# Layer 2 attention: six products of bf16 parts in 48 rows, two heads in the two halves of TensorE's rows

## The reference, cut to what matters

```
qkv = x @ w_qkv
q, k, v = split(qkv, 3)                 # each to (B=2, H=16, S=1024, dh=8)
q, k = rope(q), rope(k)
scores = einsum('bhqd,bhkd->bhqk', q, k) * dh ** -0.5
scores = where(tril(ones(S, S)), scores, finfo.min)
out = einsum('bhqk,bhkd->bhqd', softmax(scores), v)
return out @ w_out
```

## Time and profile before

| | |
|---|---|
| Runs | median 1307.3 us of 3 (1306.64 to 1309.63) |
| Profiled execution | 1312.35 us; its span, first to last instruction, 1311.1 us |
| TensorE busy over the span | 957.8 us (73%) |
| VectorE busy over the span | 916.1 us (70%) |
| ScalarE busy over the span | 570.3 us (43%) |
| Mean granted TensorE clock | 0.852 |
| Layer 2 attention, first maxima matmul to last pv | 545.5 to about 846 us |

### The profile page before, as it was taken

How to read it: one execution, slowest core, us unless ns; L and a number is a source line. 1 busy time by engine, 2 the same in 40 slices (tenths; PEclk the granted TensorE clock), 3 DMA queues, 4 the chain that set the end, 5 groups by cost and what they waited for, 6 DMA issues and landing times.

```text
span 1311.1 us, 18576 instructions
## 1 busy us (share of the span) xinstructions
PE 957.8 (73%) x5191; PEld 568.2 (43%) x5191; DVE 916.1 (70%) x1714; ACT 570.3 (43%) x1212; POOL 554.6 (42%) x553
## 2 busy tenths in 40 slices
PE   6957787878665866589999998768897381258782
PEld 3412233333344542233444433248897250247682
DVE  7599999999899557477777774184444579982223
ACT  3264564566032343216666666524343481123222
POOL 2037996899401324211111111125543487225553
PEclk9868998999778887559999999758999595659897
DMA  8000000000000300720221110051111100011113
GB/s 282 0 0 1 0 0 1 1 0 1 1 0 1 129 1 0 160 43 17 41 39 36 28 36 2 0 227 38 38 34 38 51 1 1 0 36 42 39 34 111
DMA packets 28689, 49.45 MB, mean 38 GB/s; under 512 B 7856, under 2 KB 15544, under 8 KB 27568
## 3 DMA queue, kind: packets, MB, share of 16 engines
q1 hardware_dynamic: 23344, 37.81, 10.2%
q0 software_dynamic: 4096, 8.35, 2.0%
q10 hardware_dynamic: 1152, 2.10, 0.4%
HBM read 37.61 MB, written 12.58 MB: 38 GB/s over the span
## 4 chain that ended last, share of the span: by engine, by line
PE 44%; DVE 29%; issue 10%; ACT 6%; POOL 5%; DMA 3%; SPq 1%; another core or an unknown queue 0%; DVEq 0%; ACTq 0%; POOLq 0%
PE ps L2710 9%; PE ps L1734 6%; PE ps L1719 5%; PE ps L2719 5%; PE ps L1671 5%; POOL sb_gs L889 4%; DVE sb_hs L750 3%; DVE sb_l_mxp L1848 2%; DVE sb_xn L168 2%; DVE sb_stats L145 2%; PE ps L588 1%; ACT sb_l_rc L2140 1%; PE ps L1675 1%; PE ps L471 1%; DVE sb_l_pr L2260 1%
## 5 line engine op out<-in xcount | busy, mean ns | idle before, releaser
L1848 DVE TENSOR_REDUCE sb_l_mxp<-ps 128x2 f32<-128x1024 f32 (+3 forms) x152 | 173.8, 1166 | 62.4 <-PE ps L1671 60.3
L889 POOL TENSOR_TENSOR sb_gs<-sb_hs,sb_xp 128x512 f32<-128x512 f32 x128 | 161.4, 1280 | 28.7 <-DVE sb_hs L750 26.4
L1791 ACT ACTIVATE sb_l_pT<-ps 128x512 f32<-128x512 f32 (+3 forms) x256 | 113.2, 506 | 97.5 <-PE ps L1719 94.9
L2710 PE MATMUL ps<-sb_hT,sb_f_shared 128*128 x936 | 127.4, 288 | 13.9 <-ACT sb_f_shared L2727 6.7
L588 PE MATMUL ps<-sb_gs,sb_ident 128*128 128x512 f32 x256 | 133.7, 605 | 1.0 <-POOL sb_gs L889 0.7
L2710 PEld LDWEIGHTS ps<-sb_hT,sb_f_shared 128*128 128x128 f32 x936 | 116.4, 200 | 22.9 <-issue 22.8
L2780 DVE SCALAR_TENSOR_TENSOR sb_f_rows<-ps,sb_f_mask,sb_f_rows 128x128 f32 x78 | 27.3, 351 | 114.5 <-PE ps L2719 50.2
L2808 POOL DMA_INDIRECT moe_y<-sb_f_rows,sb_f_rowi x64 | 64.1, 1002 | 81.8 <-DVE sb_f_rows L2780 71.2
L2719 PE MATMUL ps<-sb_sw_f_out,sb_f_hid 128*128 x624 | 86.6, 283 | 11.4 <-issue 10.1
L849 ACT ACTIVATE sb_xp<-ps 128x512 f32<-128x512 f32 x96 | 57.2, 596 | 85.6 <-POOL sb_gs L889 62.3
L2749 ACT ACTIVATE sb_f_hid<-ps 128x512 f32<-128x512 f32 x78 | 46.5, 596 | 100.8 <-PE ps L2710 80.9
(11 more groups left out here) (400 smaller groups left out, 2116.4 us busy)
## 6 DMA issues: line engine op xcount, KB each, us to landing
sb_sw_f_in<-w_f_in SPq DMA_DIRECT2D x2, 2048.0 KB, 9.8
sb_sw_f_out<-w_f_out SPq DMA_DIRECT2D x2, 2048.0 KB, 12.7
sb_l_qk<-spill SPq DMA_DIRECT2D x18, 192.0 KB
sb_l_qk<-spill SPq DMA_DIRECT2D x54, 64.0 KB
spill<-sb_l_parts SPq DMA_DIRECT2D x12, 256.0 KB, 4.3
moe_y<-c_f_zero SPq DMA_DIRECT2D x1, 2048.0 KB, 9.8
sb_sw_f_up<-w_f_up SPq DMA_DIRECT2D x1, 2048.0 KB, 13.1
moe_h<-sb_f_rows SPq DMA_DIRECT2D x8, 256.0 KB, 4.8
```

The source lines that it names most:

```text
L889: gp.tensor_tensor(gs[:, q % SL, :], hs[:, q % SL, :], cs[:, k % 2, hf * CH:(hf + 1) * CH], ALU.mult).then_inc(times_c, 1)
L1791: ac.activation(pT[e % 3][:, h, 0:width], ps[:, 4 + n_bank % 3, 0:width], ACT.Exp, scale=L2_SCALE).then_inc(exped, 1)
L1848: dv.tensor_reduce(dst, src, AX_X, ALU.max).then_inc(max_out, 1)
L2710: m = pe.matmul(ps[:, 2 * (i % 2) + n, fs], own[:, i % 2, n, fs], xr[:, bass.ds(r, 1), :], start=True, stop=True)
```

## The change

Of the nine products only six are kept: part a of q with part d of k for a + d of at most 2 (`PARTS`). They fill R = 48 rows, 51 with the maxima's rows. Two heads of a set now lie side by side, one from partition 0 and one from partition 64 (HALF), in two slots each, so that a set's matmuls come in pairs: the same slot and tile, rows 0 to 50 for one head and rows 64 to 114 for the other. The results of a pair go to two different PSUM banks. The mask matmuls keep all 128 rows; there are two for each group that needs them. All three buffers now have storage of their own and all their ones are set ahead of the loop, one GpSimd memset over all partitions for each buffer. A stack is 18 DMAs (was 12), a set's rows of maxima 6 DMAs (was 3). The order of the steps, the groups and what VectorE reduces in each are as before.

```diff
-        R = 9 * DH
+        PARTS = [(0, 3), (1, 2), (2, 1)]
+        R = 6 * DH
+        HALF = P // 2
         HG = 4
+        SLOTS = HG // 2
...
-        qk2 = sb("l2_qk", [R + 3, 2, 2, HG, S], BF16, ctx=ctx)
-        third = parts[0:R + 3].rearrange("p j d n -> p (j d n)")[:, 0:2 * HG * S].rearrange("p (j g n) -> p j g n", j=2, g=HG)
-        qs = [qk2[:, 0, 0], qk2[:, 1, 0], third[:, 0]]
-        ks = [qk2[:, 0, 1], qk2[:, 1, 1], third[:, 1]]
+        qk3 = sb("l2_qk", [P, NB3, 2, SLOTS, S], BF16, ctx=ctx)
+        qs = [qk3[:, i, 0] for i in range(NB3)]
+        ks = [qk3[:, i, 1] for i in range(NB3)]
...
-        CONST, STACKED, MAXROW, SPILLED, MX, MP = 5, 12 * 16, 3 * 16, 6 * 16, 1, 6
+        CONST, STACKED, MAXROW, SPILLED, MX, MP = 6, 18 * 16, 6 * 16, 6 * 16, 1, 6
...
-                def score(bank, col, width, h, t, key, start, stop):
-                    return pe.matmul(ps[:, b0 + bank, col:col + width], qs[i][0:R, h, t * P:(t + 1) * P],
-                                     ks[i][0:R, h, key:key + width], start=start, stop=stop)
...
+                def both(col, width, slot, t, key, start, stop):
+                    for half in range(2):
+                        rows = slice(half * HALF, half * HALF + R)
+                        m = pe.matmul(ps[:, b0 + half, col:col + width], qs[i][rows, slot, t * P:(t + 1) * P],
+                                      ks[i][rows, slot, key:key + width], start=start, stop=stop)
                     return m
+                def masks(blocks):
+                    for half in range(2):
+                        out = ps[:, b0 + half, :].rearrange("p (u n) -> p u n", n=P)[:, 0:HG:blocks, :]
+                        pe.matmul(out, idb[:], tri[:].unsqueeze(1).to_broadcast([P, HG // blocks, P]), start=True, stop=False)
...
-                    _, t, _, key, width, pair = group
-                    for h in range(2):
-                        m = score(h, 0, width, 2 * pair + h, t, key, True, True)
+                    _, t, _, key, width, slot = group
+                    m = both(0, width, slot, t, key, True, True)
...
-                    pe.matmul(ps[:, 4 + n_sc % 3, 0:width], ks[i][0:R + 3, h, kt * P:(kt + 1) * P],
-                              qs[i][0:R + 3, h, q0:q0 + width], start=True, stop=True).then_inc(sc_mm, 1)
+                    rows = slice(h % 2 * HALF, h % 2 * HALF + R + 3)
+                    pe.matmul(ps[:, 4 + n_sc % 3, 0:width], ks[i][rows, h // 2, kt * P:(kt + 1) * P],
+                              qs[i][rows, h // 2, q0:q0 + width], start=True, stop=True).then_inc(sc_mm, 1)
...
-                            gp.memset(ks[0][64:R + 3], 1.0).then_inc(const, 1)
+                            gp.memset(ks[0], 1.0).then_inc(const, 1)
...
-            gp.memset(ks[1][64:R + 3], 1.0).then_inc(const, 1)
+            gp.memset(ks[1], 1.0).then_inc(const, 1)
...
+            gp.memset(ks[2], 1.0).then_inc(const, 1)
+            gp.wait_ge(const, CONST)
...
-                sp.wait_ge(const, 1 if s == 0 else 3)
+                sp.wait_ge(const, (1, 3)[s] if s < 2 else CONST)
...
-                for a in range(3):
-                    rows = slice(a * 3 * DH, (a + 1) * 3 * DH)
-                    src = spill[0, h0:h0 + HG].rearrange("g d r n -> (d r) g n")[:, :, b * S:(b + 1) * S]
-                    sp.dma_start(qs[i][rows], src).then_inc(stacked[i], 16)
-                    for d in range(3):
-                        rows = slice((a * 3 + d) * DH, (a * 3 + d + 1) * DH)
-                        sp.dma_start(ks[i][rows], at(1, a)).then_inc(stacked[i], 16)
+                for half in range(2):
+                    heads = slice(h0 + half, h0 + HG, 2)
+                    r0 = half * HALF
+                    for d, n in PARTS:
+                        rows = slice(r0, r0 + n * DH)
+                        src = spill[0, heads, 0:n].rearrange("g d r n -> (d r) g n")[:, :, b * S:(b + 1) * S]
+                        sp.dma_start(qs[i][rows], src).then_inc(stacked[i], 16)
+                        src = spill[1, heads, d].rearrange("g r n -> r g n")[:, :, b * S:(b + 1) * S]
+                        for a in range(n):
+                            sp.dma_start(ks[i][r0 + a * DH:r0 + (a + 1) * DH], src).then_inc(stacked[i], 16)
+                        r0 += n * DH
...
                     for a in range(3):
-                        dst = qs[s % NB3][R + a:R + a + 1].rearrange("a g (t n) -> a (g t) n", t=TPB)
-                        sp.dma_start(dst, mp[:, s % 2, a, :]).then_inc(max_row[s % NB3], 16)
+                        for half in range(2):
+                            r0 = half * HALF + R + a
+                            dst = qs[s % NB3][r0:r0 + 1].rearrange("a g (t n) -> a (g t) n", t=TPB)
+                            src = mp[half * SLOTS * TPB:(half + 1) * SLOTS * TPB, s % 2, a, :]
+                            sp.dma_start(dst, src).then_inc(max_row[s % NB3], 16)
```

More of the change, by code:

```diff
@@ L1684, in maxima @@
                 if group[0] == "diagonals":
-                    diagonals(0, group[1])
-                    m = diagonals(1, group[2])
+                    masks(1)
+                    for slot in range(SLOTS):
+                        for u in range(2):
+                            t = group[1 + u]
+                            m = both((2 * slot + u) * P, P, slot, t, t * P, False, slot == SLOTS - 1 and u == 1)
                 elif group[0] in ("first", "tail"):
                     t = group[1]
-                    diagonals(0, t)
-                    for h in range(HG):
-                        m = score(1, h * P, P, h, t, 0 if group[0] == "first" else CH, True, True)
+                    masks(2)
+                    for slot in range(SLOTS):
+                        both(2 * slot * P, P, slot, t, t * P, False, slot == SLOTS - 1)
+                    for slot in range(SLOTS):
+                        m = both((2 * slot + 1) * P, P, slot, t, 0 if group[0] == "first" else CH, True, True)
                 elif group[0] == "all":
                     _, t, _, key = group
-                    for h in range(HG):
-                        m = score(h // 2, h % 2 * 256, 256, h, t, key, True, True)
-                else:
-                    _, t, _, key, width, pair = group
-                    for h in range(2):
-                        m = score(h, 0, width, 2 * pair + h, t, key, True, True)
+                    for slot in range(SLOTS):
+                        m = both(slot * 256, 256, slot, t, key, True, True)
+                else:
+                    _, t, _, key, width, slot = group
+                    m = both(0, width, slot, t, key, True, True)
                 m.then_inc(max_mm, 1)
@@ L1830, in reduce_group @@
                 z, b0 = s % 2, n % 2 * 2
-                blocks = ps[:, b0:b0 + 2, :].rearrange("p k (h n) -> p k h n", h=HG)
+                blocks = ps[:, b0:b0 + 2, :].rearrange("p k (s u n) -> p (k s) u n", s=SLOTS, u=2)
                 if group[0] == "diagonals":
                     _, ta, tb = group
-                    dst, src = mxp[:, z, 0, :, ta:tb + 1:tb - ta].rearrange("p h t -> p t h"), blocks
+                    dst, src = mxp[:, z, 0, :, ta:tb + 1:tb - ta], blocks
                 elif group[0] in ("first", "tail"):
                     step = 1 if group[0] == "first" else 2
-                    dst, src = mxp[:, z, 0:step + 1:step, :, group[1]], blocks
+                    dst, src = mxp[:, z, 0:step + 1:step, :, group[1]].rearrange("p a h -> p h a"), blocks
                 elif group[0] == "all":
@@ L1840, in reduce_group @@
                     dst = mxp[:, z, part_, :, t]
-                    src = ps[:, b0:b0 + 2, :].rearrange("p k (h n) -> p (k h) n", h=2)
+                    src = ps[:, b0:b0 + 2, :].rearrange("p k (s n) -> p (k s) n", s=SLOTS)
                 else:
-                    _, t, part_, _, width, pair = group
-                    dst, src = mxp[:, z, part_, 2 * pair:2 * pair + 2, t], ps[:, b0:b0 + 2, 0:width]
+                    _, t, part_, _, width, slot = group
+                    dst, src = mxp[:, z, part_, slot::SLOTS, t], ps[:, b0:b0 + 2, 0:width]
                 dv.wait_ge(max_mm, n + 1)
@@ L1928, in gpsimd @@
             for step in steps:
-                if step[0] == "stack" and step[1] == 2:
-                    for b in range(B):
-                        gp.wait_ge(spilled[b], SPILLED)
-                    gp.memset(ks[2][64:R + 3], 1.0).then_inc(const, 1)
-                    gp.wait_ge(const, CONST + 1)
-                elif step[0] == "score" and step[4] == HG - 1:
+                if step[0] == "score" and step[4] == HG - 1:
                     _, _, qc, kt, _, _, _ = step
@@ L1943, in gpsimd @@
                 elif step[0] == "project":
-                    if step[1] == 0:
-                        gp.wait_ge(const, CONST + 1)
                     gp.wait_ge(masked, n_masked)
```

8 lines of the change are left out of this document (removed).

## The result

The changed kernel takes 1297.62 us (median of 4 runs) where the kernel before took 1308.47 in the same comparison: ratio 0.9896, interval 0.9854 to 0.9938, so faster by 10.9 us. The prediction was 1281, faster by 26.7. The profiled execution took 1296.92 us, its span 1295.7.

What follows compares the result with a forecast made beforehand. TensorE was taken as the bound, 87% of a set in use. The terms -30 - 4.5 - 4 + 1.8 + 2 + 3 + 5 = -26.7 us took 1307.3 to 1281 us, range 1263 to 1304.

Steps and rivals of the forecast that it cites:

- changes of tiling: Switches between 128 and 64 rows in a set: 14 at 0.1 us, 1.4 us a set, bounds 0 and 2.8.
- the second stage: Maxima and scores both running: a set falls from 31.89 to 27.5 us, saving 30 us, bounds 21 and 44.
- V: The prediction's step that VectorE, needing 24.5 us a set, becomes the bound and sets the pace of a set.
- L: Follow-up theory for a set: the round trip TensorE to ScalarE and back through three score banks sets the pace.
- the start: First maxima come earlier because the first stack is smaller: -4.5 us, bounds 0 and -8.5.
- C: Rival: the halves do not overlap, maxima and scores keep 7.7 us each; 1315 us, chance 0.10.
- D: Rival: overlap is there but dear, TensorE needs 24 us, a set takes about 30; 1298 us, chance 0.13.
- the first stage with its rows of maxima: Maxima alone before the outputs: -4 us from faster groups, +1.8 us from three more DMA issues.
- rows of maxima in later sets: Six DMA issues a set leave less time for landing before the scores: +2 us, bounds 0 and 11.
- clock in the second stage: Pauses of TensorE bring two stretches at the lower clock level: +5 us.
- The tail: Only outputs left: pairs gain 0, the clock falls more often, +3 us, bounds 0 and 8.
- B: Rival: the clock in the second stage alternates between levels and gives the gain back; 1292 to 1322 us, chance 0.15.

Runs made afterwards that it cites:

- e12: Changed kernel with ScalarE's exponentials (from the second set on) and VectorE's reductions both halved; 1269.06 us beside 1324.98 for the kernel before, 27.43 us a set.
- e1: Changed kernel with VectorE reducing only half of the columns of each block of maxima; 1283.9 us.
- e2: Changed kernel without groups of maxima after the first set, on TensorE and VectorE; 1324.26 us.
- e3: Changed kernel with each pv of 256 or more columns split in two by columns; 1282.24 us, ratio 0.9829.
- e8: Changed kernel with split pv and maxima 1.4 sets ahead in place of 1.3; 1280.35 us, ratio 0.9723.
- e11: Changed kernel with ScalarE taking the exponential of only half of each score tile from the second set on; 1282.35 us beside 1324.98.
- e10: Changed kernel with split pv, groups of maxima kept away from pv, and maxima 1.5 sets ahead; 1290.92 us, ratio 0.9823.
- e13: e10 with VectorE reducing only half of each maxima bank; 1265.54 us beside 1324.98, a set 28.68 us where 30.07.
- e7: Changed kernel with only the lead changed, maxima 1.4 sets ahead in place of 1.3; 1278.9 us beside 1283.39, ratio 0.9968.
- e4: Kernel before with six products only, 48 rows, all heads from partition 0, no pairs; fastest run 1416.86 us where before took 1314.9.

## Why the prediction was right or wrong

The direction held, and the result lies in the range; the gain was 10.9 us of 26.7. What TensorE spends in a set at clock 1.00, as the distance from each matmul's start to the next start, waits included, summed over the timeline by line (us):

| | prediction | before, 630.57 to 662.46 | after, 655.49 to 685.63 | e12 |
|---|---|---|---|---|
| scores | 3.9 | 10.4 | 10.2 | 8.2 |
| maxima | 3.9 | 9.1 | 6.8 | 6.2 |
| pv | 9.4 | 9.4 | 9.4 | 9.4 |
| masks | 1.7 | 1.7 | 2.3 | 2.3 |
| transposes | 1.0 | 1.2 | 1.4 | 1.3 |
| changes of tiling | 1.4 | | (in the rows above) | |
| sum | 21.3 | 31.9 | 30.1 | 27.4 |

**The step that failed** is the second stage, "-30 us": "So I take a pair as one matmul: maxima and scores go from 7.7 to 3.9 us each", and from it VectorE as next bound and a set of 27.5. For maxima the pair holds: 29 of the 72 maxima matmuls of a set start within 20 ns of the one before. Their row is 6.8 and not 3.9 us in part because it holds the wait of whatever follows a group: three times 0.50 to 0.67 us pass before the fourth score of a tile, once 0.76 before a pv. Of the 48 scores only 8 start within 4 ns of the one before; the others follow after 53 to 718 ns or with other work between them. Two causes can be told apart. The order of the steps, kept as it was, puts a group of maxima inside 8 of the 24 pairs. Of the 16 left, all 8 first pairs of a tile (heads 0 and 1) start together and no second pair (heads 2 and 3) does: head 3 needs the bank that the tile's first exponential gives back, and ScalarE gives the three banks back one at a time. So the scores took 10.2 us of TensorE after 10.4 before.

The bound that took over is no engine but the ring score, exponential, pv. The prediction had described it, for the tail alone ("The fourth score waits for the first exponential, then pv, then the next first score; a pair shortens none of these"); the earlier trace rows gave its 2.47 us for a tile of 512, and with the 2.21, 1.78 and 1.56 of the narrower tiles in the same tail the 12 tiles of a set would have shown a floor near 27 us before anything else is put in. What doesn't fit into the ring's gaps adds to it: mask groups, "rows" and transposes, 30.14 in all. The stage of 6.88 sets at 31.89 - 30.14 = 1.75 gives 12.0 us, not 30; one set lost 3.6 of it, and with some gain at the stage's two ends 9.8 were measured.

**V** is refuted by e1. That the ring sets the pace is borne out by e2 at the upper clock (outputs alone are hardly faster), by e3 and e8 (shorter absences, -1.5 and -1.3 us) and by e11 (shorter exponentials). L alone is not the whole: e10 against e13 shows the second coupling, through VectorE's banks. What no run tried is the ring's own size, a fourth bank for the scores, or an order with no group inside a pair.

**Right:** the start (-4.5 predicted, -5.2 measured from first issue to first mask); the overlap itself, so C fails. The Trainium skill's rule behind C (TensorE: Matmul & The Clock Gate, Part 3, What overlaps and what doesn't), that weight loads overlap running matmuls only where row groups differ, is not what this trace shows: with a load for each block, the next pair of blocks in the same rows started 53 ns after the one before. Changes of tiling cost no more than predicted, as far as their rows show it: masks and transposes together rose by 0.8 us, 1.4 were allowed. So D, whose 1298 us came out, is wrong in its mechanism.

**Luck:** the first stage with its rows of maxima, -2.2 predicted (-4 + 1.8) and -2.4 measured. Both terms were too large and cancel. The groups, first reduction to "rows", went from 27.6 to 25.4 us, 2.3 in place of 4. The rows cost almost nothing: the three issues more took their time (3.74 us for six), but from the start of "rows" to the first score it is 7.4 us after 7.2, since that score came 1.2 us after the last issue had ended, and 3.0 us in the kernel before.

**Sizes:** rows of maxima in later sets (+2) and clock in the second stage (+5) are one event: at 639.66 a first score waits 0.99 us for these DMAs, at 642.0 the clock falls for 6.8 us, and that set takes 33.76. The tail was +0.8 for +3, with the clock at 0.50 for 13.5 us in it. That the wait brought the fall is not shown by itself; in e7 both are gone together. B's alternation didn't come in this kernel; e2 shows how near it is.

**Open:** why e4's clock stays low, what holds the 6.1 us by which e12's set exceeds the prediction's 21.3 (in the table, scores 4.3 and maxima 2.3 more), why a longer lead alone makes sets 0.33 us longer (e7), and how much of the remaining 28.8 us of e8 each coupling holds.

## What to carry to other kernels

When the full engine is relieved, look for the next bound among rings as well as engines: a few buffers passed between two in-order engines have a period of their own, and a stretch of the trace in which only that ring runs shows it. Matmuls side by side save time only where they follow each other in the program and their results have room at the same moment. And work taken from TensorE can cost its clock, as in e2, so an experiment that leaves work out must be read with the granted clock beside it.

## What the runs showed of the hardware that was not expected

The granted clock stayed at 0.50 while TensorE streamed matmuls over 48 and 51 rows without pause (e4: 40.00 of 40.00 us busy by the modelled ends). The kernel before, with 72 and 75 rows, was as busy at 0.50 (10.00 of 10.00 us, second row) and had 1.00 right after. With pairs over both halves the clock stood at 1.00 with TensorE busy 26.78 of 30.14 us, and in e8 for 198 us on end. But e4 too had 1.00 for a time, from 847.5 to 878.2 us. Why it differs from the kernel before was not tested.

The two matmuls of a pair start 3 to 4 ns apart, and two scores of 512 columns together take 0.22 us, as one alone.
